# Weights taken already transposed, split by long instructions on three engines, in a transformer block with routed experts

## The reference

```python
x = x + 0.5 * ffn(layernorm(x), ...)
x = x + attn(layernorm(x), ...)         # 16 heads, causal
x = x + 0.5 * ffn(layernorm(x), ...)    # the same weights again
```

```python
def _expert(h, g, u, d):                # g, u: (352, 128); d: (128, 352)
    return einsum('...i,hi->...h', silu(h @ g.T) * (h @ u.T), d)
logits = x @ wr.T + rb                  # (tokens, 7)
probs = softmax(logits); scores, idx = top_k(probs, 2); scores /= scores.sum()
out = shared_out + sum_e w[..., e] * _expert(x, rg[e], ru[e], rd[e])
```

## Time and profile before

| | us |
|---|---|
| median of three runs | 596.37 (594.8 to 597.38) |
| the profiled execution | 592.31 |
| its span, first to last instruction | 590.6 |
| share of the span: PE / DVE / ACT / POOL busy | 92% / 77% / 56% / 43% |
| mean granted TensorE clock | 0.98 |

### The profile page before, as it was taken

How to read it: one execution, slowest core, us unless ns; L and a number is a source line. 1 busy time by engine, 2 the same in 40 slices (tenths; PEclk the granted TensorE clock), 3 DMA queues, 4 the chain that set the end, 5 groups by cost and what they waited for, 6 DMA issues and landing times. The chain is left out here.

```text
span 590.6 us, 11873 instructions
## 1 busy us (share of the span) xinstructions
PE 543.8 (92%) x3738; PEld 431.3 (73%) x3738; DVE 453.5 (77%) x1151; ACT 331.0 (56%) x701; POOL 254.8 (43%) x400
## 2 busy tenths in 40 slices
PE   1898999998895779999999999999999999999996
PEld 1778999997783546666666666666655889999995
DVE  3679868779548899797979797979564888777965
ACT  4454444446643527676767676768777434444543
POOL 7387856445342161111111212121236888864440
PEclk9999999999997989999999999999999999999997
DMA  9931435941563356222222222220000121341314
GB/s 244 290 83 38 122 80 145 234 126 48 162 197 110 114 155 162 82 87 83 88 86 84 90 80 86 86 88 10 4 2 24 32 78 52 101 110 59 107 38 113
DMA packets 46889, 58.74 MB, mean 99 GB/s; under 512 B 6183, under 2 KB 37678, under 8 KB 46062
## 3 DMA queue, kind: packets, MB, share of 16 engines
q1 hardware_dynamic: 38160, 46.77, 28.2%
q0 software_dynamic: 4480, 9.25, 4.9%
q10 hardware_dynamic: 4190, 1.98, 1.3%
HBM read 38.09 MB, written 28.00 MB: 112 GB/s over the span
## 5 line engine op out<-in xcount | busy, mean ns | idle before, releaser
L1771 DVE TENSOR_REDUCE mxp<-psum 128x1 f32<-128x512 f32 (+3 forms) x304 | 179.5, 655 | 30.3 <-PE psum L1617 29.4
L1830 ACT ACTIVATE probs<-psum 128x512 f32<-128x512 f32 (+1 forms) x304 | 155.1, 578 | 41.2 <-PE psum L1660 38.1
L1660 PE MATMUL psum<-queries,keys 128*128 128x512 f32 (+3 forms) x384 | 122.4, 381 | 0.5 <-DMA queries<-m_rows 0.3
L1617 PE MATMUL psum<-keys,queries 128*128 128x512 f32 (+1 forms) x304 | 115.3, 414 | 1.3 <-DVE mxp L1771 0.9
L1877 POOL TENSOR_SCALAR_AFFINE_SELECT probs<-probs 128x512 f32<-128x512 f32 x64 | 39.9, 634 | 175.5 <-ACT probs L1830 175.4
L1177 POOL DMA_INDIRECT y_rows<-ys,to_row x76 | 74.4, 979 | 81.4 <-DVE ys L1085 53.7
L996 ACT ACTIVATE silu<-psum 128x352 f32<-128x352 f32 x107 | 49.7, 464 | 102.6 <-PE psum L890 101.3
L1041 DVE TENSOR_TENSOR act<-silu,psum 128x352 f32<-128x352 f32 x107 | 55.5, 519 | 46.2 <-ACT silu L996 45.4
L1660 PEld LDWEIGHTS psum<-queries,keys 128*128 128x128 f32 x384 | 66.7, 190 | 26.7 <-ACT probs L1830 12.6
L1689 PE MATMUL psum<-probs,vg 128*32 128x512 f32 (+3 forms) x768 | 69.8, 491 | 0.4 <-POOL probs L1877 0.4
L1617 PEld LDWEIGHTS psum<-keys,queries 128*128 128x128 f32 x304 | 57.9, 193 | 15.0 <-DVE mxp L1771 4.8
(11 more groups left out here) (260 smaller groups left out, 1020.5 us busy)
## 6 DMA issues: line engine op xcount, KB each, us to landing
z_rows<-q_stack SPq DMA_DIRECT2D x12, 682.5 KB, 5.2
keys<-q_stack SPq DMA_DIRECT2D x12, 512.0 KB, 10.3
keys<-k_stack SPq DMA_DIRECT2D x32, 128.0 KB, 6.3
queries<-q_stack SPq DMA_DIRECT2D x8, 512.0 KB, 6.0
zg_early<-z_rows SPq DMA_DIRECT2D x44, 65.0 KB, 1.9
yc<-y_rows SPq DMA_DIRECT2D x10, 256.0 KB, 3.9
zg_late<-z_rows SPq DMA_DIRECT2D x32, 65.0 KB, 2.1
k_stack<-zt_h SPq DMA_DIRECT2D x8, 256.0 KB, 3.0
```

What stands on the lines that cost most here:

```text
L1617: ins = e.matmul(dst, K.queries[u][:, i * P:(i + 1) * P], K.keys[u][:, heads[0]:heads[-1] + 1, k0 * P:(k0 + nb) * P], start=True, stop=Tru ...
L1660: ins = e.matmul(slot(K, u, d, n)[:, m * (q1 - q0):(m + 1) * (q1 - q0)], K.keys[v][:, j, kt * P:(kt + 1) * P], K.queries[v][:, q0:q1], sta ...
L1771: e.tensor_reduce(K.mxp[:, heads[0]:heads[-1] + 1, i, which], scores, AX.X, ALU.max).then_inc(K.A["taken"], 1)
L1830: e.activation(probs_of(K, product)[:, heads[0]:heads[-1] + 1, :], src, ACT.Exp, scale=SCALE).then_inc(K.A["ex"], 1)
```

## The change

The host lays the weights out as the kernel wants them (`laid_out`): gate and up with the 128 inputs on the partitions, down in three blocks of 128 hidden rows padded with zeros, the router's weights and the middle third of the attention weights transposed. All 24 groups of weight transposes on PE go, and with them the two small ones ahead (the router's weights, and a third of the attention's). The splitting is cut into ten pieces instead of 24 groups, with sources in SBUF instead of PSUM: shared gate, up, down (352, 352, 384 columns); routed gate and up in two pieces each (three experts, 1056 columns, and four experts, 1408 columns), whose subtractions now run on POOL; and routed down in three pieces of 896 columns. Order of the ten: ACT casts the three shared ones behind the norm's hi of chunks 0 and 1, then z of chunks 2 and 3, then the four gate/up pieces, then silu of tile 0; the three down pieces follow at steps 0 to 2.

```diff
+WEIGHTS = [(w, slice(0, 1)) for w in ("g", "u", "d")] + \
+          [(w, slice(x0, x1)) for w in ("g", "u") for x0, x1 in ((1, 4), (4, EXPERTS))] + [("d", k) for k in range(3)]
+SHARED_WEIGHTS = 3
+POOL_WEIGHTS = [3, 4, 5, 6]
+LATE_WEIGHTS = [7, 8, 9]
-AWAKE = [{0: 2, 1: 3}, {}]
+AWAKE = [{}, {}]
+def weights_lo(K, e, m, done):
+    w, src, hi, lo = (WEIGHTS[m][0],) + weights_of(K, m)
+    e.wait_ge(K.w_hi, m + 1)
+    if w != "d":
+        e.tensor_tensor(lo, src, hi.bitcast(F32), ALU.subtract).then_inc(done, 1)
+    else:
+        e.scalar_tensor_tensor(lo, src, 0.5, hi.bitcast(F32), ALU.mult, ALU.subtract).then_inc(done, 1)
```

On PE, tile 0's `up_pe` stands right behind the logits of chunks 0 and 1:

```diff
             norm_tr_pe(K, 0, 0)
             norm_tr_pe(K, 0, 1)
             logits_pe(K, 0, 0, 0)
             logits_pe(K, 0, 0, 1)
-            norm_tr_pe(K, 0, 2)
-            norm_tr_pe(K, 0, 3)
-            weights_pe(K, 0)
-            places_pe(K, 0, 0)
-            ...
             ffn_pe(K, 0)
```

and the rest goes into the tables of the loop (`tr0`, `hi0`, `lo0`, `logits0`: the norm's transposes, hi, lo and the logits of chunks 2 and 3):

```diff
+BETWEEN_PE = [{0: (("tr0", 2),), 1: (("places", 0), ("tr0", 3)), 3: (("logits0", 2),), 4: (("logits0", 3),)}, ...
+BETWEEN_ACT = [{0: (("hi0", 2),), 1: (("hi0", 3),), ...
+BETWEEN_DVE = [{0: (("lo0", 2),), 1: (("lo0", 3),)}, ...
+BEHIND_DVE = [{1: (("weights_lo", 7),), 2: (("weights_lo", 8),), 3: (("weights_lo", 9),), 13: (("small", 0),), ...
-FRONT_PE = {4: (("places", 1),), ...
+FRONT_PE = {9: (("places", 1),), ...
+FRONT_DVE = {4: (("segments", 0),), 5: (("lists", (0, 0)), ("lists", (0, 1)), ("lists", (0, 2)), ("lists", (0, 3))),
+             6: (("router", (1, 0)),), 7: (("router", (1, 1)),), 10: (("places", 1),), 11: (("segments", 1),),
+             12: (("lists", (1, 0)),), 13: (("lists", (1, 1)),), 14: (("lists", (1, 2)),), 15: (("lists", (1, 3)),)}
```

DVE's prelude ends with the three shared subtractions, both parts of the router for the first half, and `places_dve` for it; `act_dve` of tile 0 stands behind them. POOL runs its four subtractions between the norm's part and the first scatter:

```diff
             for c in range(NCH):
                 norm_rstd_pool(K, 0, c)
+            for m in POOL_WEIGHTS:
+                weights_lo(K, e, m, K.w_lo_pool)
             sort_part_pool(K, 0, 0)
```

and the memset behind each scatter of the first ffn's sorting goes:

```diff
-    if f == 0 or g % TT > 0:
+    if f == 1 and g % TT > 0:
         pause_pool(K, f == 1 and t < HALF)
```

More of the change, by code:

```diff
@@ L267 @@
 R_BANKS = [[R_BANK, R_BANK], [EARLY_BANKS[0], R_BANK]]
-TP_FREE = [max((p + 1 for p in range(m) if TP_BANK[p] == TP_BANK[m]), default=0) for m in range(NTP)]
 N_CONST = 6
-N_CONST2 = 7
+N_CONST2 = 6
 N_SPARES = 4
@@ L435, in place_memory @@
     K.psum = ctx.enter_context(K.nc.psum_tensor("psum", [P, 8, CHUNK], F32))
-    K.ld = {n: sem(f"ld_{n}") for n in ("nat", "nat2", "small", "bias", "const", "out")}
+    K.ld = {n: sem(f"ld_{n}") for n in ("shared", "g", "u", "d", "small", "bias", "const", "out")}
     K.ld_x = [sem(f"ld_x{b}") for b in range(BATCH)]
@@ L558, in norm_tr_pe @@
     e.wait_ge(K.NS[k]["z"], c + 1)
-    if c > 1:
+    if k == 0 and c == 3:
+        e.wait_ge(K.NS[k]["lo"], c)
+    elif c > 1:
         e.wait_ge(K.NS[k]["lo"], c - 1)
@@ L1454, in weights_hi_act, with small_sources @@
[L1454 to L1458, removed]
-    else:
-        K.nc.scalar.copy(hi, src).then_inc(K.tp_hi, 1)
+    e.wait_ge(K.padded, 1)
+    for w, src in small_sources(K):
+        e.copy(K.small[w + "h"][:, :], src).then_inc(K.sw_hi, 1)
+    e.copy(K.rw[:, 0:NGATE], K.nat_route[:, :]).then_inc(K.sw_hi, 1)
+def small_sources(K):
+    return [(w, K.nat_attn[:, k * EMB:(k + 1) * EMB]) for k, w in enumerate("qkv")] + [("p", K.nat_proj[:, :])]
@@ new lines, in weights_of @@
+def weights_of(K, m):
+    w, part = WEIGHTS[m]
+    wall = K.wall[:, :].rearrange("p (x c) -> p x c", c=WCOLS)
+    if w != "d":
+        hi, lo = (GH, GL) if w == "g" else (UH, UL)
+        return K.nat[w][:, part, :], wall[:, part, hi:hi + HID], wall[:, part, lo:lo + HID]
+    down = wall[:, :, DN:].rearrange("p x (k a m) -> p x k a m", a=2, m=EMB)
+    if m < SHARED_WEIGHTS:
+        return K.nat[w][:, :, 0, :], down[:, 0, :, 0, :], down[:, 0, :, 1, :]
+    return K.nat[w][:, part, 1:, :], down[:, 1:, part, 0, :], down[:, 1:, part, 1, :]
@@ new lines, in weights_hi_act @@
+def weights_hi_act(K, m):
+    e, w = K.nc.scalar, WEIGHTS[m][0]
+    src, hi, _ = weights_of(K, m)
+    if m < SHARED_WEIGHTS:
+        e.wait_ge(K.ld["shared"], 16 * 3)
+    else:
+        e.wait_ge(K.ld[w], 16)
+    if w == "d":
+        e.activation(hi, src, ACT.Copy, scale=0.5).then_inc(K.w_hi, 1)
+    else:
+        e.copy(hi, src).then_inc(K.w_hi, 1)
+def weights_lo(K, e, m, done):
+    w, src, hi, lo = (WEIGHTS[m][0],) + weights_of(K, m)
+    e.wait_ge(K.w_hi, m + 1)
+    if w != "d":
+        e.tensor_tensor(lo, src, hi.bitcast(F32), ALU.subtract).then_inc(done, 1)
+    else:
+        e.scalar_tensor_tensor(lo, src, 0.5, hi.bitcast(F32), ALU.mult, ALU.subtract).then_inc(done, 1)
@@ L1856, in attn_act @@
     e = K.nc.scalar
-    e.wait_ge(K.A["ready"], 1)
+    e.wait_ge(K.A["ready"], 2)
     for c in range(2, NCH):
@@ L2123, in late_pe @@
         up_pe(K, f, c, 0)
+    elif step == "tr0":
+        norm_tr_pe(K, 0, c)
+    elif step == "logits0":
+        logits_pe(K, 0, 0, c)
     elif step == "n_tr":
@@ L2142, in late_act @@
         norm_z_act(K, 2, c)
+    elif step == "hi0":
+        norm_hi_act(K, 0, c)
+    elif step == "weights":
+        weights_hi_act(K, c)
     elif step == "tanh":
@@ L2173, in late_dve @@
         norm_z_dve(K, 2, c)
+    elif step == "lo0":
+        norm_lo_dve(K, 0, c)
+    elif step == "small":
+        weights_small_dve(K)
+    elif step == "weights_lo":
+        weights_lo(K, K.nc.vector, c, K.w_lo)
     elif step == "norm_lo":
```

168 lines of the change are left out of this document (53 added, 115 removed).

## The result

The changed kernel takes 620.78 us (median of 4 runs, 619.64 to 622.0), the kernel before in the same comparison 596.88: ratio 1.0403, 95% interval 1.0363 to 1.0443. I had said 593.1 with a range of 584 to 598, so this is outside, on the side to which I gave the smallest chance. The profiled execution took 622.0 us; the one of before 592.31, so 29.7 us are to be explained, and 33 against my sum.

What follows compares the result with a forecast made beforehand. PE was taken to bound the kernel, 94% busy behind 90.9 us. Milestones 2.5, 3.6, 4.1 and finally 3.3 us early at batch 3 gave 592.31 - 3.3 = 589.0 profiled, 593.1 on the median's scale; range 584 to 598.

Steps and rivals of the forecast that it cites:

- the side to which I gave the smallest chance: The whole kernel getting slower, chance 0.16, against faster 0.51 and same 0.33.
- my sum: The whole profiled execution: 592.31 less 3.3 us, giving 589.0 us.
- Part 1: The start: POOL's subtractions hold up DVE's router instructions, yet tile 0's product starts at 34.8, 2.5 us early.
- rival A: The start: the lock of POOL and DVE bites little, 12.0 us gained in all, 584.4 us; chance 0.25.
- Part 2: Tile 0 to tile 2: takes 2.7 us instead of 3.85, tile 2 starts at 37.5, 3.6 us early.
- One tile at the low clock, + 0.8: Tile 2 runs at PE's lower clock after the idle stretch, costing 0.8 us.
- Part 3: Tile 2 to tile 13: takes 31.7 us instead of 32.2, tile 13 at 69.2, 4.1 us early.
- Part 4: First sort's scatters: without memsets 1.13 us each, first half free, batch 3 at 87.6, 3.3 us early.
- rival B: First sort: without memsets DVE and POOL lock each other, batch 3 is 4.2 us later, 600.6 us; chance 0.15.
- From batch 3 on nothing changed is on PE's path: Behind batch 3's transposes: the 3.3 us gained there reach the end unchanged.

Runs made afterwards that it cites:

- e6: The changed kernel with POOL's four weight subtractions moved behind its first half of scatters; 1.0348 of the kernel before.
- e8: As e6, with the memset behind each scatter of the first sort put back; 1.01 of the kernel before.
- e12: The changed kernel with memsets back, POOL's four subtractions on DVE, and the second half's router and places at earlier steps; 0.9999 of the kernel before.
- e15: The changed kernel without an edit, run again on chip A; 1.009 of the kernel before.
- e15c: The changed kernel without an edit, run again on chip D; 1.0043 of the kernel before.
- e2: The changed kernel with forty 512-column matmuls behind tile 1's gate and up matmuls, chip A; 1.0112 of the kernel before.
- e7: As e6, with sixteen 512-column matmuls behind tile 1's gate and up matmuls; 1.0453 of the kernel before.
- e1: The changed kernel with the memset behind each scatter of the first sort put back, chip A; 1.011 of the kernel before.
- e5: The changed kernel without an edit, run again on chip B; 1.0411 of the kernel before.
- e13: As e12, with four 512-column matmuls behind the gate and up matmuls of tiles 5 to 11, chip A; 0.9998 of the kernel before.
- e4b: The kernel before without the memsets behind its first sort's scatters, a second time, chip A; 0.9978 of the kernel before.
- e10: As e9, without the memsets; 1.0313 of the kernel before.
- e2b: The kernel of e2 again, unedited, on chip C; 1.0482 of the kernel before.
- e9: The changed kernel with memsets back and POOL's four weight subtractions done by DVE behind tiles 5, 6, 8 and 9; 1.009 of the kernel before.

## Why the prediction was wrong, step by step

**Part 1, the lock: right.** 11.04 us of subtractions against 11.1, four router instructions held up as forecast, tile 0's product at 34.54 against 34.8. The match is closer than the working: 20.6 + 11.1 is 31.7, not the 32.3 that I wrote, and POOL began at 19.80, 0.8 us earlier than I had it. e6 confirms the price, 9.0 us at tile 2 where rival A had 8.7. The Trainium skill's rule in SBUF — State Buffer, "Who interferes with whom", agrees with what was seen here: the DVE instructions that waited beside the subtractions had two SBUF inputs, and POOL was reading SBUF. But I took from L1779's one instance that a DVE instruction gets through between two of POOL's; e8's L735 waited for four. DVE does the same pieces in 1.25 + 1.62 = 2.87 us (e12) where POOL takes 5.57 for two. The Trainium skill's GPSIMD Engine Reference, "Engine selection", has GpSimd about twice as slow as VectorE for two-input elementwise work; the trace agrees, with 1.94 times here.

**Part 2: right in its time (37.18 against 37.5), wrong in one term.** "One tile at the low clock, + 0.8": that is about what e15 and e15c paid, where the higher clock was back at about 40 and 41 us; in the profiled execution it was tiles 2 to 5, and 6 to 7 us more for the same program. The idle stretch was in my text, and the trace of before had no case of a return from one this long; I should have given this term a range. I had also put the removed `AWAKE` matmuls at 0. No run shows otherwise: e2 and e7, with more of them in the same wait, lost the clock as well.

**Part 3: right where no stall comes.** Tile 2 to 13 in e15c takes 32.6 us against 31.7; with stalls 53.9.

**Part 4: the step that failed.** I wrote that the scatters of the first half are "free" and that each saves 0.3 to 0.4 us: I priced the memset by its own duration on POOL. What its absence does to the others I looked for only as a lock between DVE and POOL (rival B: its place was PE idle ahead of batch 3, its price 4.2 us). That closely spaced scatters slow engines which do not wait for them is a cost that I had put at nothing. Measured: 14.6 and 15.3 us in the two pairs that differ by the memsets alone, on chips B and C; on A no harm (e15 at 1.009 without them, e1 at 1.011 with them). For the first comparison the stall is inferred, not tested: its trace has the same late signals in much the same places as e5's, and against e15c, the same program, the profiled execution is 25.0 us later at tile 21, of which 6.4 is the clock in tiles 2 to 5. In e5 the clock came back as in e15c (tile 5 at 48.75 and 48.97), and tile 21 is 23.4 us later than there: the stall alone.

**"From batch 3 on nothing changed is on PE's path": wrong.** SP's queue carried the lateness of the second half's rows past batch 3 into the results' loads, 3.1 us in e15c. With it that execution is 0.65 us behind before at tile 53, and 2.4 at the end. Nearly all of the last 1.8 us arises in the second ffn, whose code hardly changed; the cause stays open. e12 and e13 are 2.9 and 4.6 us early at tile 53 and have nothing of it left at the end. About 3 us of that arise up to the second ffn's tile 1, at a granted clock of 0.96 against 0.98, and e4b, without the change, has the same 0.96 there; so it is not shown that the change has a part in them. The rest stays open.

So on a chip without stalls the change is a small loss of 0.4 to 0.9%: the 3 us that the start gains are back before the end. In the first comparison and on chip B, where it stalls, it is 4%; on C only variants of it ran, e10 and e2b, at 1.031 and 1.048. What stays open of the stall: by what path POOL's scatters delay other engines' signals, why two of four chips (or groups of runs) are spared, whether the memset or only the wider spacing protects, and whether the kernel before would stall without its memsets.

## What to carry to other kernels

A short instruction that does nothing useful may be there for its neighbours. Price its removal by what it separates, and try the removal alone, on more than one chip, with the unchanged kernel beside it in every group; without that control I read three runs of a spared chip as three cures. And two-input elementwise work on GpSimd beside a dependent chain of two-input VectorE instructions costs the chain its whole length: here 9 us of waiting for 11 us of work that VectorE does in about 6.

## What I had not expected of the hardware

- While GpSimd issues indirect scatters 1.27 us apart, TensorE, VectorE and ScalarE wait 3 to 8 us at a time for signals of each other that were due, on some chips, with the DMA engines about 16% busy. At 1.56 us apart, with a 0.43 us memset between, no such wait of 2 us or more was seen in e8, e9 and e12 on the same chips.
- The same program is at 1.041 of the kernel before on one chip and at 1.004 on another; the intervals reach 0.8 and 0.3 per cent to either side.
- TensorE, fully busy behind the same idle stretch, returned to its higher clock after about 5 us in one execution of the changed kernel (e15c) and after 19 in another (the first).
- A VectorE instruction that takes 0.29 us alone lasted 11.07 us beside GpSimd's four subtractions (e8).
